# Three quads of score blocks in place of four in the attention layer of a four-layer graph network

## The chip, the cores and the metric

The program runs on one core of one Trainium2 chip. The metric is the device time of one launch in microseconds (us), the median of three runs. The core's engines are TensorE (PE in the rows: matrix products), VectorE (DVE), ScalarE (ACT), GpSimd (POOL, idle here) and SyncE (SP), which issues the transfers.

## The reference, cut to what matters

Four layers work on `x` (4096 rows of 256 features) and one dense adjacency matrix of 4096 x 4096. Each normalises its input first and adds its output to `x`. The change concerns the last one, a graph attention:

```
h   = inp @ W
e   = leaky_relu(h @ a1 + (h @ a2).T, 0.2)              # 4096 x 4096 scores, u_i + v_j
att = softmax(where(adj > 0,  e, -1e12), axis=1)
neg = -softmax(where(adj > 0, -e, -1e12), axis=1)
out = elu(concat(att @ inp, neg @ inp) @ wtrans)
```

`inp` is the normalised and clipped `x`. Everything is computed in float32 in this layer.

## The kernel before, in words

The first three layers and the preparation of the fourth take the first 1396 us of the execution. The attention then goes over eight chunks of 512 output rows (`NC = 8`, `CH = 512`). A chunk has two passes: quads 0 to 7 for the softmax of the scores, quads 8 to 15 for that of the negated scores (`QPH = 8`, `QPC = 16`). A quad covers four tiles of 128 input rows, so it is four score blocks of 128 x 512 float32 that lie side by side (8 KB in each partition). Every quad is made and used in the same place, in five steps:

1. ScalarE, `scores` (L683): four instructions that put the leaky sum of `u` and `v` into the four blocks.
2. VectorE (L1102): subtracts the row's shift.
3. VectorE (L1118): adds the mask exponents, which are zero or hugely negative.
4. ScalarE (L691): the exponential.
5. TensorE (L1370): 16 products of 128x128 by 128x257, which the trace shows as 32 records. They add to four banks of PSUM. The 257th column sums the exponentials.

The blocks come from a ring of quads, `quads`. Before step 1 may write into a quad of the ring, TensorE must have ended the products of the quad that used it last: that is the wait for `p_used` in `scores`. ScalarE's order is fixed by the code: the exponential of quad k, then the scores of quad k + 2, then the exponential of quad k + 1, and so on.

Other work stands between these steps, in written order:

- VectorE, between steps 2 and 3 of a quad, runs one search for the largest or smallest score in half a row of `adj` (L1016, L1020). There are 16 a chunk. Quads 0 to 4 serve rows of the next chunk, with that numbering shifted so that quads 11 to 15 already serve the chunk after it. At quad 3 it waits for a row load that SP issues behind a mask load. The last chunk has no searches, and the one before it none from quad 11.
- VectorE has a few more pieces of work in a chunk: the reciprocals of the row sums at quad 3 (of the chunk before) and quad 11, the sum of the two halves at quad 5 (L1061, L1063), the residual at quad 8 (L1072, L1073), and the next chunk's shifts in front of quad 11 (L1031 to L1042).
- ScalarE converts masks (L426 with `big<-big`) after the scores in quads 0, 1 and 10 to 15, scales results at quads 3 and 11 (L653), copies two rows at quads 6 and 14, and runs the three ELU instructions at quad 6 (L660, L661, L663), between the scores of quad 8 and the exponential of quad 7.
- TensorE spreads two columns over the partitions (L1221, 1.78 us) in front of quads 4 and 12.
- SP issues mask loads (L343) and row loads (L346) in one fixed sequence. A mask load waits until ScalarE has converted the mask that its buffer held, and all that stands behind it in the sequence waits with it.

Of the kernel before, what the change touches and what calls it, by code (L numbers as in the profile page):

```python
# [21 lines left out]
P = 128  # L22


def gnn_stack(nc, x_in, adj_t, adj, w_gcn, b_gcn, w_conv1, w_conv2, w_gcn2, b_gcn2,
# [7 lines left out]
    CH = 512  # L33
# [8 lines left out]
    YW = F + 1  # L42
    QD = 4
    QPH = NT // QD
    QPC = 2 * QPH
# [18 lines left out]
    with ctx:  # L64
        def sb(name, shape, dt):
            return ctx.enter_context(nc.sbuf_tensor(name, shape, dt))
# [5 lines left out]
        Y_WORDS = NT * 2 * YW  # L72
        big = sb("big", [P, Y_WORDS + NT * CH], f32)
        feat = sb("feat", [P, NT * F], f32)
        work = sb("work", [P, 10240], f32)

        def words(t, lo, n):
            return t[:, lo:lo + n]
# [21 lines left out]
        Yb = words(big, 0, Y_WORDS).rearrange("p (j s f) -> p j s f", j=NT, s=2)  # L100
# [2 lines left out]
        wt_sb = words(work, 8192, 1024).rearrange("p (k f) -> p k f", k=FB)  # L103
        t_row = words(work, 0, 4096)
        quads = [words(t, lo, QD * CH).rearrange("p (s n) -> p s n", s=QD)
                 for t, lo in ((work, 4096), (work, 4096 + QD * CH), (big, Y_WORDS + 12288), (big, Y_WORDS + 14336))]
        RING = len(quads)
        R = words(work, 8192, 2 * TPC * F).rearrange("p (s t f) -> p s t f", s=2, t=TPC)
        rows = words(feat, 0, 2 * HALF).rearrange("p (s n) -> p s n", s=2)
# [38 lines left out]
        ps = ctx.enter_context(nc.psum_tensor("ps", [P, 8, 512], f32))  # L148
# [47 lines left out]
        def wait(eng, s, v):  # L196

            if not isinstance(v, int) or v > 0:
                eng.wait_ge(s, v)
# [224 lines left out]
        def _(act):  # L424
# [202 lines left out]
            def rows_copy(s, n):  # L627

                act.wait_ge(ab_ps_ready, n)
                copy(AB[:, 2 * s:2 * s + 2, :], ps[:, 4 * s:4 * s + 2, :]).then_inc(ab_ready, 1)  # L630
# [14 lines left out]
            def averages(c, s):  # L645

                act.wait_ge(rz_ready, c * 2 + (s + 1))
                if s == 0:
                    wait(act, fin_out, c * 16)
                else:  # L650
                    wait(act, fin_ready, c)
                for t in range(TPC):
                    nc.scalar.activation(R[:, s, t, :], ps[:, 4 * s + t, 0:F], ACT.Copy, scale=rz[:, s, t:t + 1])\  # L653
                      .then_inc(att_evac, 1)
# [18 lines left out]
            def scores(c, k):  # L673

                s, q = k // QPH, k % QPH
                slots = quads[k % RING]
                if q == 0:
                    act.wait_ge(ab_ready, c * 2 + s + 1)
                if not (isinstance(c, int) and c == 0 and k < RING):
                    act.wait_ge(p_used, c * QPC + (k - RING + 1))  # L680
                for t in range(QD):
                    j = q * QD + t
                    ins = nc.scalar.activation(slots[:, t, :], AB[:, 2 * s, :], ACT.Prelu, bias=v_col[:, j:j + 1],  # L683
                                               alpha=ALPHA)
                ins.then_inc(edge_ready, 1)

            def att_chunk(c, first, last):
                for k in range(QPC):
                    act.wait_ge(lin_ready, c * QPC + k + 1)
                    slots = quads[k % RING]  # L690
                    nc.scalar.activation(slots, slots, ACT.Exp, scale=1.0 if k < QPH else -1.0).then_inc(p_ready, 1)  # L691
                    if k == 3 and not first:
                        averages(c - 1, 1)
                    if k == 6:
                        wait(act, lin_ready, c * QPC)
                        rows_copy(1, c * 2 + 2)
                    if k == QPH + 3:
                        averages(c, 0)
                    if k == QPC - 2 and not last:
                        rows_copy(0, c * 2 + 3)  # L700
                    if k + 2 < QPC:
                        scores(c, k + 2)
                    elif not last:
                        scores(c + 1, k + 2 - QPC)
                    if first and k + 2 < QPH:
                        mask_exponents(c, k + 2)
                    if not first and k < 2:
                        mask_exponents(c, k + QPH - 2)
                    if not last and QPH + 2 <= k:
                        mask_exponents(c + 1, k - QPH - 2)  # L710
                    if k == 6 and not first:
                        elu_exp(c - 1)
                    if k == QPH and not first:
                        store_result(c - 1)
                        load_x3(c)
# [23 lines left out]
        def _(dve):  # L739
# [85 lines left out]
            for c in range(NC):  # L825
                for g in range(GROUPS):
# [17 lines left out]
                    if g in (6, 8, 10, 12):  # L844
                        t = (g - 6) // 2
# [140 lines left out]
            for c in range(NC):  # L986
                dve.wait_ge(vb_evac, c + 1)
                nc.vector.tensor_reduce(vext[:, 0, c:c + 1], t_row[:, c * CH:(c + 1) * CH], AX.X, ALU.max)
                ins = nc.vector.tensor_reduce(vext[:, 1, c:c + 1], t_row[:, c * CH:(c + 1) * CH], AX.X, ALU.min)
# [99 lines left out]
            def att_chunk(c, ch, first, last):  # L1089
                for k in range(QPC):  # L1090
                    s, q = k // QPH, k % QPH
                    slots = quads[k % RING]
                    if k == SHIFT and not last:
                        shifts(c + 1, ch)
                    if q == 0:
                        dve.wait_ge(ab_ready, c * 2 + (s + 1))
                    found = searches(c, k, first, last)
                    for c_m, m in found:
                        if m % 2 == 0:
                            dve.wait_ge(row_in[m // 2 % 2], (c_m * TPC + m // 4) * 16 + 16)  # L1100
                    dve.wait_ge(edge_ready, c * QPC + k + 1)
                    nc.vector.tensor_tensor(slots, slots, AB[:, 2 * s + 1:2 * s + 2, :].to_broadcast([P, QD, CH]),  # L1102
                                            ALU.subtract).then_inc(shifted, 1)
                    for c_m, m in found:
                        dve.wait_ge(row_used, c_m * SEARCHES + m)
                        extreme(m // 4, m // 2 % 2, m % 2)
                    if k == 3 and not first:
                        reciprocals(c - 1, 1, ch)
                    if k == QPH + 3:
                        reciprocals(c, 0, ch)  # L1110
                    if k == 5 and not first:
                        summed(c - 1, ch)
                    if k == QPH and not first:
                        with_residual(c - 1, ch)
                    if s == 0:
                        dve.wait_ge(mask_ready, c * NC + (q + 1))
                    dve.wait_ge(shifted, c * QPC + k + 1)
                    nc.vector.tensor_tensor(slots, slots, mask[:, q * QD:(q + 1) * QD, :],  # L1118
                                            ALU.add if s == 0 else ALU.subtract).then_inc(lin_ready, 1)
# [36 lines left out]
            for t in range(TPC):  # L1156
# [3 lines left out]
                ins = nc.vector.tensor_tensor(D, D, M, ALU.add)  # L1160
# [5 lines left out]
        def _(pe):  # L1166
            mm = nc.tensor.matmul
# [3 lines left out]
            for k in range(FB):  # L1171
                for f in range(FB):
                    ins = mm(ps[:, 3, 2 * k:2 * k + 2], w3t_sb[:, f, k * P:(k + 1) * P], a_sb[:, f, :],
                             start=(f == 0), stop=(f == FB - 1))
# [18 lines left out]
            for c in range(NC):  # L1193
# [5 lines left out]
                for g in range(GROUPS):  # L1199
                    pe.wait_ge(cast16_done, c * GROUPS + g + 1)  # L1200
                    for jj in range(PANELS):
                        for t in range(TPC):
                            ins = mm(deg[:, t:t + 1], piece16[:, g % 2, jj, t * P:(t + 1) * P], ones16[:, :],
                                     start=False, stop=False, skip_group_check=True)
# [19 lines left out]
            for l in range(4):  # L1224
# [80 lines left out]
                if l == 3:  # L1305

                    pe.wait_ge(wa_ready, 1)
                    for k in range(2):
                        for f in range(FB):
                            ins = spread(ps[:, 4, k * F + f * P:k * F + (f + 1) * P], wa_sb[:, f, k:k + 1])  # L1310
# [46 lines left out]
            def att_chunk(c, last):  # L1357
                for k in range(QPC):
                    s, q = k // QPH, k % QPH
                    if q == 0:  # L1360
                        pe.wait_ge(ab_ready, c * 2 + (s + 1))
                    if k == 4:
                        spread_rows(1, c)
                    if k == QPH + 4 and not last:
                        spread_rows(0, c + 1)
                    pe.wait_ge(p_ready, c * QPC + k + 1)
                    for jj in range(QD):
                        j = q * QD + jj
                        for t in range(TPC):
                            ins = mm(ps[:, 4 * s + t, 0:YW], quads[k % RING][:, jj, t * P:(t + 1) * P], Yb[:, j, s, :],  # L1370
                                     start=(j == 0), stop=(j == NT - 1), skip_group_check=True)
                    ins.then_inc(p_used, 1)

# [3 lines left out]
            for c in range(NC):  # L1377
                if c >= 2:
                    pe.wait_ge(vb_evac, c - 1)
                for t in range(TPC):  # L1380
                    ins = spread(ps[:, 6 + c % 2, t * P:(t + 1) * P], uv_sb[:, c * TPC + t, 1:2])
# [5 lines left out]
            for j in range(NT):  # L1387
# [3 lines left out]
                if j == NT // 2:  # L1391
                    pe.wait_ge(hsum_ready, 1)
                    for k in range(FB):
                        ins = mm(ps[:, 5, :], hsum1[:, k:k + 1].to_broadcast([P, P]), wt_sb[:, k, :],
                                 start=(k == 0), stop=(k == FB - 1), skip_group_check=True)
# [40 lines left out]
```

## Time and profile before

| | |
|---|---|
| median of 3 runs | 2328.44 us (2327.26 to 2329.3) |
| the profiled execution | 2330.11 us, its span 2328.3 us |
| TensorE's matmuls | busy 2146.7 us, 92% of the span |
| VectorE | busy 1428.3 us, 61% |
| ScalarE | busy 1530.4 us, 66% |
| chain that ended last | TensorE 84%, transfers 7%, VectorE 5% |

Busy shares are means over layers with different limits. For the change only the stretch from 1396 us to 2318 us counts. The times in the rows are from the start of the span. An instruction on VectorE or ScalarE can begin a little before the one ahead of it has ended, so the pace of an engine is read from start to start.

### The profile page before, as it was taken

How to read it: one execution, taken by the hardware profiler on the slowest of the kernel's cores; microseconds unless marked ns; L12 is line 12 of the kernel's file. 1: busy time of each engine (PE TensorE's matmuls, PEld its weight loads, DVE VectorE, ACT ScalarE, POOL GpSimd, SP SyncE). 2: the span in 40 equal slices, each digit the busy share in tenths (PEclk: the TensorE clock that was granted, in tenths of full speed). 3: DMA queues.
4: the chain of work that ended last, by engine and by line, in shares of the span. 5: the costliest groups of instructions: out<-in, count | busy, mean ns of one | idle time of the engine just before them, and what ended most of it. 6: DMA issues, size and time to landing. Idle time of an engine off the chain costs nothing.

```text
span 2328.3 us, 27448 instructions
## 1 busy us (share of the span) xinstructions
PE 2146.7 (92%) x10872; PEld 1475.1 (63%) x10980; DVE 1428.3 (61%) x2241; ACT 1530.4 (66%) x1780; POOL 1.9 (0%) x12
## 2 busy tenths in 40 slices
PE   2665899999998999999999869999999999999998
PEld 1332455555555555554555528888888888888887
DVE  4777543410001423342444869999999999999774
ACT  6777555565655756556665447878787969696974
POOL 0000000000000000000000000000000000000000
PEclk9876999999999999999999989999999999999999
DMA  8999111310003011032112465445444535352300
GB/s 292 314 314 322 52 53 53 109 55 19 19 10 109 1 55 55 28 115 74 54 34 84 143 219 199 165 143 180 138 170 145 172 136 181 127 194 96 109 19 9
DMA packets 152992, 277.29 MB, mean 119 GB/s; under 512 B 6688, under 2 KB 79136, under 8 KB 144672
## 3 DMA queue, kind: packets, MB, share of 16 engines
q1 hardware_dynamic: 144416, 267.15, 33.8%
q10 hardware_dynamic: 8448, 8.39, 1.1%
q8 instruction: 86, 1.41, 0.2%
q14 instruction: 42, 0.34, 0.0%
HBM read 241.96 MB, written 33.55 MB: 118 GB/s over the span
## 4 chain that ended last, share of the span: by engine, by line
PE 84%; DMA 7%; DVE 5%; ACT 2%; issue 2%; POOL 0%; DVEq 0%; SPq 0%; ACTq 0%; POOLq 0%
PE ps L1370 37%; PE ps L1243 35%; PE ps L1268 8%; DMA work<-in_adj_t 6%; PE ps L1188 2%; ACT work L426 1%; PE ps L1221 1%; DVE feat L1016 1%; DMA feat<-in_adj 1%; PE ps L1253 1%; DVE feat L1020 1%; DVE hsum L1004 0%; PE ps L1343 0%; DVE big L829 0%; ACT big L426 0%
## 5 line engine op out<-in xcount | busy, mean ns | idle before, releaser
L1243 PE MATMUL ps<-work,feat 128*128 128x512 bf16 x3686 | 815.7, 379 | 11.3 <-DVE feat L876 4.3
L426 ACT ACTIVATE work<-big 128x1024 bf16<-128x1024 uint8 x472 | 496.1, 1055 | 265.2 <-PE ps L1243 261.6
L1243 PEld LDWEIGHTS ps<-work,feat 128*128 128x128 f16 x3776 | 369.1, 98 | 446.7 <-issue 6.8
L1370 PE MATMUL ps<-big,work 128*128 128x257 f32 x2048 | 451.8, 381 | 17.9 <-ACT work L691 17.9
L1370 PE MATMUL ps<-big 128*128 128x257 f32 x2048 | 449.4, 380 | 2.9 <-ACT big L691 2.9
L1370 PEld LDWEIGHTS ps<-big,work 128*128 128x128 f32 x2048 | 389.0, 191 | 74.1 <-issue 18.7
L1370 PEld LDWEIGHTS ps<-big 128*128 128x128 f32 x2048 | 388.3, 190 | 58.9 <-ACT big L691 3.7
L1268 PE MATMUL ps<-work 128*128 128x256 f32 x896 | 199.0, 379 | 4.5 <-ACT work L426 4.5
L1268 PEld LDWEIGHTS ps<-work 128*128 128x128 f32 x896 | 169.9, 190 | 32.0 <-ACT work L426 6.5
L426 ACT ACTIVATE work<-work 128x1024 bf16<-128x1024 f32 x129 | 134.6, 1052 | 80.2 <-DMA work<-in_adj_t 52.8
L691 ACT ACTIVATE work<-work 128x2048 f32<-128x2048 f32 x64 | 122.2, 1910 | 87.7 <-DVE work L1118 87.7
L691 ACT ACTIVATE big<-big 128x2048 f32<-128x2048 f32 x64 | 122.0, 1906 | 78.2 <-DVE big L1118 77.4
L907 DVE TENSOR_REDUCE gmax<-work 128x1 f32<-128x256 f32 x32 | 11.8, 414 | 263.3 <-ACT work L529 263.3
L683 ACT ACTIVATE big<-feat 128x512 f32<-128x512 f32 x256 | 163.1, 710 | 15.5 <-PE ps L1370 15.5
L683 ACT ACTIVATE work<-feat 128x512 f32<-128x512 f32 x256 | 163.3, 712 | 10.0 <-PE ps L1370 9.5
L917 DVE SCALAR_TENSOR_TENSOR work<-ps,dsc,work 128x256 f32<-128x256 f32 x64 | 31.0, 484 | 226.0 <-PE ps L1268 224.3
L1102 DVE TENSOR_TENSOR work<-work,feat 128x2048 f32<-128x2048 f32 x64 | 146.2, 2285 | 34.1 <-ACT work L683 33.6
L1102 DVE TENSOR_TENSOR big<-big,feat 128x2048 f32<-128x2048 f32 x64 | 146.3, 2285 | 23.4 <-ACT big L683 17.9
L1016 DVE CUSTOM_DVE_ANT_0 feat<-feat,work 128x2048 uint8<-128x2048 f32 x64 | 146.2, 2284 | 4.3 <-DMA feat<-in_adj 3.8
L426 ACT ACTIVATE work<-ps 128x1024 f32<-128x1024 f32 (+1 forms) x64 | 61.0, 954 | 131.3 <-PE ps L1268 111.2
L1118 DVE TENSOR_TENSOR work<-work,big 128x2048 f32<-128x2048 f32 x64 | 146.3, 2286 | 0.5
L1020 DVE CUSTOM_DVE_ANT_0 feat<-feat,work 128x2048 uint8<-128x2048 f32 x64 | 146.2, 2285 | 0.5
(147 smaller groups left out, 1479.6 us busy)
## 6 DMA issues: line engine op xcount, KB each, us to landing
work<-in_adj_t SPq DMA_DIRECT2D x128, 512.0 KB, 5.4
feat<-in_adj SPq DMA_DIRECT2D x64, 1024.0 KB, 7.2
big<-in_adj_t SPq DMA_DIRECT2D x64, 1024.0 KB, 5.3
h_spill<-work SPq DMA_DIRECT2D x32, 512.0 KB, 4.2
feat<-h_spill SPq DMA_DIRECT2D x32, 512.0 KB, 4.1
x_spill<-work SPq DMA_DIRECT2D x24, 512.0 KB, 3.0
work<-in_x SPq DMA_DIRECT2D x16, 512.0 KB, 5.3
work<-x_spill SPq DMA_DIRECT2D x16, 512.0 KB, 3.9
```

What stands on the lines that cost most here:

```text
L426: return nc.scalar.activation(out_, in_, ACT.Copy, **kw)
L683: ins = nc.scalar.activation(slots[:, t, :], AB[:, 2 * s, :], ACT.Prelu, bias=v_col[:, j:j + 1], alpha=ALPHA)
L691: nc.scalar.activation(slots, slots, ACT.Exp, scale=1.0 if k < QPH else -1.0).then_inc(p_ready, 1)
L917: nc.vector.scalar_tensor_tensor(y_t, o_t, dsc[:, bass.ds(i0 + t, 1)], bias_row, ALU.mult, ALU.add).then_inc(out_used[l], 1)
L1016: nc.vector.tensor_tensor_reduce(out=junk, in0=rows[:, h, :], in1=t_row[:, h * HALF:(h + 1) * HALF], scale=1.0, scalar=0.0, op0=ALU.mult, ...
L1020: nc.vector.tensor_tensor_reduce(out=junk, in0=rows[:, h, :], in1=t_row[:, h * HALF:(h + 1) * HALF], scale=1.0, scalar=-1.0, op0=ALU.subtr ...
L1102: nc.vector.tensor_tensor(slots, slots, AB[:, 2 * s + 1:2 * s + 2, :].to_broadcast([P, QD, CH]), ALU.subtract).then_inc(shifted, 1)
L1118: nc.vector.tensor_tensor(slots, slots, mask[:, q * QD:(q + 1) * QD, :], ALU.add if s == 0 else ALU.subtract).then_inc(lin_ready, 1)
L1188: ins = mm(ps[:, bank + f, :], parts[:, j, h, f * P:(f + 1) * P], stage0[:, n % 2, jj, :], start=(j % (NT // 2) == 0 and h == 0), stop=(j ...
L1243: ins = mm(ps[:, bank + f, :], parts[:, j, h, f * P:(f + 1) * P], stage[:, g % STAGES, jj, :], start=(fresh and h == 0), stop=(end and h = ...
L1268: ins = mm(out_slot(t), T_sb[:, k, t * P:(t + 1) * P], w_sb[:, k, :], start=(k == 0), stop=(k == KB[l] - 1), skip_group_check=True)
L1370: ins = mm(ps[:, 4 * s + t, 0:YW], quads[k % RING][:, jj, t * P:(t + 1) * P], Yb[:, j, s, :], start=(j == 0), stop=(j == NT - 1), skip_gro ...
```

## The change

The ring gets three quads; the fourth one, at the end of `big`, is no longer used. Since 16 quads a chunk are not a multiple of three, the place of a quad in the ring is now counted over all chunks. The wait in `scores` follows the ring's length: the scores of quad k + 2 now wait for the products of quad k - 1, where they waited for those of quad k - 2.

```
-                 for t, lo in ((work, 4096), (work, 4096 + QD * CH), (big, Y_WORDS + 12288), (big, Y_WORDS + 14336))]
+                 for t, lo in ((work, 4096), (work, 4096 + QD * CH), (big, Y_WORDS + 12288))]
...
             def scores(c, k):
 
                 s, q = k // QPH, k % QPH
-                slots = quads[k % RING]
+                slots = quads[(c * QPC + k) % RING]
                 if q == 0:
                     act.wait_ge(ab_ready, c * 2 + s + 1)
-                if not (isinstance(c, int) and c == 0 and k < RING):
+                if c * QPC + k >= RING:
                     act.wait_ge(p_used, c * QPC + (k - RING + 1))
```

The three other uses of `quads[k % RING]`, in ScalarE's, VectorE's and TensorE's loops, become `quads[(c * QPC + k) % RING]` in the same way. No instruction is added, removed or moved.

ScalarE's first quads of the attention, before (L683 scores, L691 exponential, L426 mask; "big" and "work" are the tensors that hold the blocks):

```order
568 L683 ACTIVATE big<-feat 128x512 x4
569 L426 ACTIVATE big<-big 128x2048 [waits mask_in1]
570 L691 ACTIVATE big<-big 128x2048 [waits lin_ready]
571 L683 ACTIVATE work<-feat 128x512 [waits p_used]
572 L683 ACTIVATE work<-feat 128x512 x3
```

And the same place now:

```order
568 L683 ACTIVATE work<-feat 128x512 [waits p_used]
569 L683 ACTIVATE work<-feat 128x512 x3
570 L426 ACTIVATE big<-big 128x2048 [waits mask_in1]
571 L691 ACTIVATE big<-big 128x2048 [waits lin_ready]
572 L683 ACTIVATE work<-feat 128x512 [waits p_used]
```

The scores of quad 3 are now the first that wait for TensorE, and they go into the first block of the ring; the sequence of the instructions is the same.

## Rows read from the trace of the kernel before

**Rows 1.** Chain that ended last, in order of time: start us, us, what.
```profile
1831.54 1.78 PE ps L1221 x16
1833.32 55.48 PE ps L1370 x256
...
2234.15 83.23 PE ps L1370 x384
```
**Rows 2.** Timeline, one quad to the next: start us, us, engine, line, operation.
```profile
1798.58 2.29 DVE L1102 TENSOR_TENSOR work<-work,feat 128x2048 f32<-128x2048 f32 x1
...
1805.20 2.28 DVE L1102 TENSOR_TENSOR big<-big,feat 128x2048 f32<-128x2048 f32 x1
1805.32 1.91 ACT L691 ACTIVATE work<-work 128x2048 f32<-128x2048 f32 x1 [2.25 <-DVE work L1118]
```
**Rows 3.** Timeline, VectorE's further work at quads 11, 3, 5 and 8.
```profile
1811.82 0.15 DVE L1031 TENSOR_TENSOR feat<-feat 128x4 f32<-128x4 f32 x1
...
1813.16 2.29 DVE L1102 TENSOR_TENSOR big<-big,feat 128x2048 f32<-128x2048 f32 x1
...
1817.57 0.16 DVE L1048 TENSOR_TENSOR feat<-ps,lone 128x4 f32<-128x4 f32 x1
...
1817.86 2.26 DVE L1118 TENSOR_TENSOR big<-big 128x2048 f32<-128x2048 f32 x1
...
1872.81 0.16 DVE L1048 TENSOR_TENSOR feat<-ps,lone 128x4 f32<-128x4 f32 x1
...
1873.31 2.28 DVE L1118 TENSOR_TENSOR big<-big 128x2048 f32<-128x2048 f32 x1
...
1886.53 1.22 DVE L1061 TENSOR_TENSOR work<-work 128x1024 f32<-128x1024 f32 x1
...
1889.37 2.28 DVE L1118 TENSOR_TENSOR work<-work,big 128x2048 f32<-128x2048 f32 x1
...
1909.22 1.22 DVE L1072 SCALAR_TENSOR_TENSOR work<-feat,work 128x1024 f32<-128x1024 f32 x1
...
1911.62 2.29 DVE L1118 TENSOR_TENSOR work<-work,big 128x2048 f32<-128x2048 f32 x1
```
**Rows 4.** Timeline, quad 2 of the fifth chunk: exponential, and its products.
```profile
1866.47 1.91 ACT L691 ACTIVATE big<-big 128x2048 f32<-128x2048 f32 x1 [0.46 <-DVE big L1118]
...
1874.77 14.03 PE L1370 MATMUL ps<-big 128*128 128x257 f32 x64
```
**Rows 5.** Timeline, quads 6 and 7 of the fifth chunk: exponentials, and quad 6's products.
```profile
1898.31 1.91 ACT L691 ACTIVATE big<-big 128x2048 f32<-128x2048 f32 x1 [2.25 <-DVE big L1118]
...
1904.29 14.03 PE L1370 MATMUL ps<-big 128*128 128x257 f32 x64
...
1906.47 1.89 ACT L691 ACTIVATE big<-big 128x2048 f32<-128x2048 f32 x1
```
**Rows 6.** Timeline, start of the last chunk, where scores wait for TensorE.
```profile
2204.47 14.03 PE L1370 MATMUL ps<-big,work 128*128 128x257 f32 x64
2204.67 2.56 ACT L683 ACTIVATE big<-feat 128x512 f32<-128x512 f32 x4 [0.77 <-PE ps L1370]
...
2207.26 2.29 DVE L1102 TENSOR_TENSOR big<-big,feat 128x2048 f32<-128x2048 f32 x1 [2.25 <-ACT big L683]
```
**Rows 7.** Timeline, the row load that quad 3 of the second chunk waits for.
```profile
1513.08 2.55 ACT L683 ACTIVATE big<-feat 128x512 f32<-128x512 f32 x4
...
1517.87 0.50 SPq L346 DMA_DIRECT2D feat<-in_adj  x1
...
1525.20 2.29 DVE L1102 TENSOR_TENSOR big<-big,feat 128x2048 f32<-128x2048 f32 x1 [0.74 <-DMA feat<-in_adj]
```
**Rows 8.** Timeline, the same wait in the fifth chunk.
```profile
1868.39 2.29 DVE L1102 TENSOR_TENSOR big<-big,feat 128x2048 f32<-128x2048 f32 x1 [1.96 <-DMA feat<-in_adj]
```
**Rows 9.** Timeline, the third quad of the attention, with TensorE's wait.
```profile
1414.33 7.20 PE L1370 MATMUL ps<-big 128*128 128x257 f32 x32 [1.13 <-ACT big L691]
```
**Rows 10.** Windows: stretch, its length, busy us (count) of PE, PEld, DVE, ACT, POOL; PEclk, DMA share, GB/s.
```profile
1414.00:1423.00 9.00, 7.20 (x32) 5.99 (x32) 8.96 (x7) 6.21 (x7) 0.00 (x0) 1.00 0.66 240
```

More of the change, by code:

```diff
@@ L689, in att_chunk @@
                     act.wait_ge(lin_ready, c * QPC + k + 1)
-                    slots = quads[k % RING]
+                    slots = quads[(c * QPC + k) % RING]
                     nc.scalar.activation(slots, slots, ACT.Exp, scale=1.0 if k < QPH else -1.0).then_inc(p_ready, 1)
@@ L1091, in att_chunk @@
                     s, q = k // QPH, k % QPH
-                    slots = quads[k % RING]
+                    slots = quads[(c * QPC + k) % RING]
                     if k == SHIFT and not last:
@@ L1369, in att_chunk @@
                         for t in range(TPC):
-                            ins = mm(ps[:, 4 * s + t, 0:YW], quads[k % RING][:, jj, t * P:(t + 1) * P], Yb[:, j, s, :],
+                            ins = mm(ps[:, 4 * s + t, 0:YW], quads[(c * QPC + k) % RING][:, jj, t * P:(t + 1) * P], Yb[:, j, s, :],
                                      start=(j == 0), stop=(j == NT - 1), skip_group_check=True)
```

## The prediction, on record before the changed kernel ran

> **What bounds the kernel now.** I read the chain that ended last first, since it says whether a wait elsewhere matters at all. From 1423 us to 2317 us it is TensorE without a break: 55.48 us for eight quads, 1.78 us for a spread, again and again, and 83.23 us for the last twelve quads [rows 1]. So a quad takes TensorE 55.48 / 8 = 6.935 us, a chunk takes it 2 x (55.48 + 1.78) = 114.52 us, and any time that TensorE spends waiting in the attention is added to the end.
>
> Then I read the timeline for the engine next in line. VectorE starts one quad 6.62 us after the other [rows 2], three instructions of about 2.205 us, so 6.615 us. Its further work in a chunk, from start to start, is 1.34 and 0.29 us at quad 11, 0.50 at quad 3, 2.84 at quad 5 and 2.40 at quad 8 [rows 3], in all 7.37 us. Its chunk is thus 16 x 6.615 + 7.37 = 113.2 us of work against TensorE's 114.5. It may stand idle for only 1.3 us a chunk; beyond that the chunk grows with it, us for us. Neither engine has reserve, and what lets their uneven rhythms pass each other is the number of quads that stand finished between them.
>
> That reserve is the third thing to read. I call lead the time from the end of a quad's exponential to the start of its products. At quad 2 of the fifth chunk it is 1874.77 - (1866.47 + 1.91) = 6.4 us [rows 4]; at quad 6, behind the lump of quad 5, it is 1904.29 - (1898.31 + 1.91) = 4.1 us [rows 5]. The kernel uses several us of lead, and VectorE is hardly held back.
>
> **The change, part by part.** No instruction comes or goes, so the only term is the wait. The scores of quad k + 2 may start when TensorE has ended quad k - 1, which is when it starts quad k (or the spread in front of it). Call that start S(k).
>
> *How large the lead can then be.* In the last chunk the longer ring already binds, and its rows give the delays: the scores start 2204.67 - 2204.47 = 0.20 us after TensorE goes on to its next quad, and the shift follows 2207.26 - 2204.67 = 2.59 us behind [rows 6]. From a shift to its exponential it is 1805.32 - 1798.58 = 6.74 us with a search in between, and the exponential takes 1.91 [rows 2]. So quad k + 2 is finished at S(k) + 0.20 + 2.59 + 6.74 + 1.91 = S(k) + 11.44, and TensorE wants it at S(k) + 13.87. The lead is at most 2.43 us. Before it was 4.1 to 6.4 at the places read above, so the wait binds.
>
> *What this costs in a chunk.* Per quad VectorE gains 6.935 - 6.615 = 0.32 us of lead, and the spreads give 1.78 in front of quads 4 and 12. The lumps take it away. I follow the lead from quad 11, where it will turn out to be zero:
> - Quad 12: 0 + 1.78 + 0.32 = 2.10. Quad 13: 2.42. From quad 14 to quad 2 of the next chunk it stands at the limit, and VectorE loses 0.32 us in each of these quads, 1.6 us in all.
> - Quad 3 has a load in it. SP sends the row behind the mask load that waits for the conversion at quad 0, and that conversion stands on ScalarE behind the scores of quad 2. From the start of such scores to the row in place it was 1525.20 - 1513.08 = 12.12 us; the row was issued at 1517.87, 7.3 us before it was there [rows 7]. The scores now start at S(0) + 0.20, so the row is there at S(0) + 12.32. VectorE is free for quad 3 at S(0) + 0.20 + 2.59 + 6.62 = S(0) + 9.41: it waits 2.9 us, where it waited 0.74 to 1.96 [rows 7, 8]. Quad 3 is finished at 12.32 + 0.50 + 6.74 + 1.91 = 21.47 and wanted at 3 x 6.935 = 20.81. TensorE waits 0.66.
> - Quad 4: lead 2.10. Quad 5: 2.10 + 0.32 - 2.84, TensorE waits 0.42.
> - Quad 7: from the exponential of quad 6 to that of quad 7 ScalarE takes 1906.47 - 1898.31 = 8.16 us, with the row copy, the scores and the ELU in between [rows 5]. TensorE takes 6.94, and the lead at quad 6 is 0.32: it waits 8.16 - 6.94 - 0.32 = 0.90.
> - Quad 8: VectorE has had this time to gain, so 0.32 + 0.32 + 0.90 + 0.32 - 2.40, TensorE waits 0.54.
> - Quad 11: 0.32 x 3 - 1.34 - 0.29, TensorE waits 0.67, and the lead is zero, as assumed.
>
> The sum is 0.66 + 0.42 + 0.90 + 0.54 + 0.67 = 3.19 us a chunk. A second way gives the same: VectorE's 113.2 of work plus 1.6 plus 2.9 of idling is 117.7, which is 114.5 + 3.2. This holds for chunks 1 to 5 (counting from 0): 15.95 us. Chunk 6 has no searches from quad 11, so its last term goes: 2.52. The last chunk has no searches at all, and VectorE has 2.2 us to spare in each quad; only the ELU at quad 6 stays, between 0 and 0.9 us, and I take 0.5. Chunk 0 has none of the lumps but quad 11, and TensorE waits for VectorE in its first quads either way: 0.
>
> The sum is 19.0 us. The profiled execution would go from 2330.11 to 2349.1. It stands 1.7 us above the median, and on the median the change gives 2328.44 + 19.0 = 2347.4 us, 0.8% more.
>
> *Bounds of the terms.* The row load is the least certain. By the second way a chunk loses 113.2 + 1.6 - 114.5 = 0.3 us and the wait at quad 3 on top. If that wait stayed at the 0.74 us of before [rows 7], a chunk would lose 1.04, six of them 6.2, and with 0.5 for the last chunk the time would be 2335.1. If the load were as late as the latest of before, 1.96 against 0.74 us [rows 7, 8], each of six chunks would lose 1.2 us more than I forecast, 26.3 in all: 2354.7. I take the middle value since it is the chain of rows 7 with nothing changed but its start.
>
> *A rule against this sum.* The lead of 4.1 us and more [rows 4, 5] is what I call the reserve in use. The Trainium skill (Trainium Kernel Development and Optimization, Best Practices) asks to double-buffer for performance and names no more buffers than two; by that rule three quads suffice and the time stays at 2328.4. The lead and the 1.3 us of slack speak against it here, and I leave it as a rival.
>
> **The rivals.**
>
> 1. *The ring of three is enough.* Two quads in work and one in use would cover everything if the lumps of VectorE fell where TensorE's spreads give time. For it: over a whole chunk VectorE needs 1.3 us less than TensorE. Against it: the largest lumps (2.9 + 0.5, 2.84, 2.40) each exceed or nearly reach the limit of 2.43, and only the one at quad 5 has a spread just ahead. Time 2328, chance 0.05.
>
> 2. *Much slower: the waits feed each other.* Later scores make later mask conversions, these make later loads, and further row loads than the one at quad 3 come late; or TensorE, with five short waits in a chunk, is granted the lower clock (1.2 in place of 2.4 GHz) now and then. For the first: SP's sequence has the rows behind the masks, and a row that is 1 us later at one more quad costs up to 6 us. Against the clock: at 1414.33 TensorE started a quad behind a wait of 1.13 us, the stretch around it had it busy for only 7.20 of 9 us, and the granted clock there was 1.00 [rows 9, 10]. My waits are 0.4 to 0.9 us. Two further late rows would give 2347 + 12 = 2359. Chance of over 2357: 0.10.
>
> 3. *Faster than before.* The blocks of the fourth quad leave `big`, so a sixth of the 4096 matmul records, 683, read `work` instead (two of three quads lie there, in place of two of four). If products from `work` were faster, TensorE's chain would shorten at 683 times that difference. It decides against my waits from 19.0 / 683 = 28 ns a record, 13% of the pace of 6.935 us / 32 = 217 ns; to come out 0.2% below before it needs 35 ns. Against it: the eight quads of a half chunk, which draw equally from both tensors, keep one pace of 55.48 us, and the pairs of quads that are marked for `big` and for `work` both take 14.03 us [rows 1, 4, 6]. Time 2323, chance 0.02.
>
> 4. *A third of it.* The row at quad 3 arrives as early as before, since SP's sequence catches up in another place. For it: of the 12.12 us from scores to row only 7.3 are the transfer [rows 7]. Against it: the rest is the scores and the conversion themselves, which both stand before it still. Then the lower bound holds, 2335. Chance 0.06.
>
> **How the numbers follow.** The forecast, 2337 to 2357 us, has 0.77; rivals 1 to 4 have 0.05, 0.10, 0.02 and 0.06. The range is 2336 to 2357: it takes in nearly all between the two bounds of the row load and some us above for the last chunk and for the ELU. A measurement of this kernel can tell about 0.2%, 4.7 us, from no change. Below that by forecast is only rival 3: faster 0.02. Rival 1 is the same: 0.05. The rest, 0.93, is slower.
>
> **What the profile of the changed kernel would show.** The chain of the attention is still nearly all TensorE, but broken in chunks 1 to 6 in front of quads 3, 5, 7, 8 and 11 by VectorE and ScalarE, at 117.7 us from one chunk to the next where it was 114.5. ScalarE's scores wait for TensorE in most quads from 14 to 2, some 0.8 us each, and VectorE waits for scores there by about 0.3. The shift of quad 3 waits 2.5 to 3.5 us for its row. The granted clock stays 1.00. All durations of single instructions are as before.
>
> Wrong would be: TensorE unbroken at 114.5 us a chunk (rival 1); waits at other quads than the five; a wait at quad 3 far from 0.7 us, which would be the row load mis-sized; a lower clock in the attention; or a total outside the range with five waits of the right size in a chunk, which would put time outside the attention.

## The result, and the profile after

The changed kernel takes 2354.0 us, the median of four runs (2349.2 to 2358.7), against 2328.5 us before. The ratio is 1.011, 95% interval [1.0088, 1.0132]. Forecast were 2347.4 us and 2336 to 2357: slower, and inside the range, 6.6 us above the point. The profiled execution took 2358.71 us, 28.6 us more than that of before. One of the four later executions of the same kernel (e1 below) took 2413.7 us in a slower state of the chip, and its ratio leaves that one out.

Where the 28.6 us are is seen by cutting the execution at TensorE's first product of the attention. In the timeline that product starts at 1396.5 us before and 1402.7 us after, 6.2 us later, in layers that the change does not touch. From the first to the last product of the attention it takes 920.9 us before and 943.3 us after: 22.4 us.

The chain that ended last, from the page of the changed kernel (shares of the span, by engine and by line):

```profile
PE 67%; DVE 15%; DMA 9%; ACT 5%; issue 4%; SPq 0%; DVEq 0%; POOL 0%; ACTq 0%
```

TensorE had 84% of this chain before; the attention's unbroken piece [rows 1] is now cut by VectorE and by transfers. The timeline of chunk 2 (counted from 0) shows the cuts. Columns: start us, us, engine, line, operation, shapes, records, and in brackets the idle time ahead with what ended it. From the chunk's first product to its quad 11, and then the first products of the next chunk:

```profile
1641.45 7.10 PE L1370 MATMUL ps<-big 128*128 128x257 f32 x32
1641.65 2.56 ACT L683 ACTIVATE work<-feat 128x512 f32<-128x512 f32 x4 [0.78 <-PE ps L1370]
...
1644.12 1.89 ACT L426 ACTIVATE big<-big 128x2048 bf16<-128x2048 f32 x1
1644.24 2.29 DVE L1102 TENSOR_TENSOR work<-work,feat 128x2048 f32<-128x2048 f32 x1 [0.16 <-ACT work L683]
1645.92 1.89 ACT L691 ACTIVATE work<-work 128x2048 f32<-128x2048 f32 x1
...
1646.45 0.51 SPq L346 DMA_DIRECT2D feat<-in_adj  x1
...
1648.38 14.03 PE L1370 MATMUL ps<-big,work 128*128 128x257 f32 x64
...
1653.85 2.29 DVE L1102 TENSOR_TENSOR big<-big,feat 128x2048 f32<-128x2048 f32 x1 [2.89 <-DMA feat<-in_adj]
...
1663.03 7.20 PE L1370 MATMUL ps<-big 128*128 128x257 f32 x32 [0.62 <-ACT big L691]
...
1671.85 7.10 PE L1370 MATMUL ps<-big,work 128*128 128x257 f32 x32
...
1679.11 7.20 PE L1370 MATMUL ps<-big,work 128*128 128x257 f32 x32 [0.15 <-ACT work L691]
...
1686.14 7.10 PE L1370 MATMUL ps<-big 128*128 128x257 f32 x32
...
1693.87 7.20 PE L1370 MATMUL ps<-big,work 128*128 128x257 f32 x32 [0.63 <-ACT work L691]
...
1701.44 7.17 PE L1370 MATMUL ps<-big,work 128*128 128x257 f32 x32 [0.37 <-ACT work L691]
...
1722.81 7.20 PE L1370 MATMUL ps<-big,work 128*128 128x257 f32 x32 [0.32 <-ACT work L691]
...
1759.37 14.03 PE L1370 MATMUL ps<-big,work 128*128 128x257 f32 x64
```

The chunk lasts 1759.37 - 1641.45 = 117.92 us, where it was 114.52. The scores start 0.20 us after TensorE's new quad (1641.65), as in [rows 6]. The row is issued at 1646.45 and VectorE starts quad 3 at 1653.85: it has waited 2.89 us. TensorE then waits in front of quads 3, 5, 7, 8 and 11, and nowhere else. The brackets understate these waits, since the record of the last product runs on behind its pace. Measured from start to start, a quad of 6.94 us and a spread of 1.78 us taken off, they are 0.78, 0.32, 0.79, 0.54 and 0.48 us. Quads behind a wait also show 7.20 us in place of 7.10: TensorE loses another 0.1 us when it starts again (at quad 8, which follows a quad that waited itself, this 0.1 us is taken off too).

VectorE's row wait in quad 3 of the chunks 1 and 3 to 6, one row each from the timeline, and for chunk 3 the issue of its row:

```profile
1535.91 2.29 DVE L1102 TENSOR_TENSOR work<-work,feat 128x2048 f32<-128x2048 f32 x1 [2.89 <-DMA feat<-in_adj]
...
1764.37 0.51 SPq L346 DMA_DIRECT2D feat<-in_adj  x1
...
1773.04 2.29 DVE L1102 TENSOR_TENSOR work<-work,feat 128x2048 f32<-128x2048 f32 x1 [4.17 <-DMA feat<-in_adj]
...
1891.53 2.29 DVE L1102 TENSOR_TENSOR work<-work,feat 128x2048 f32<-128x2048 f32 x1 [3.38 <-DMA feat<-in_adj]
...
2009.23 2.29 DVE L1102 TENSOR_TENSOR big<-big,feat 128x2048 f32<-128x2048 f32 x1 [2.66 <-DMA feat<-in_adj]
...
2127.44 2.29 DVE L1102 TENSOR_TENSOR work<-work,feat 128x2048 f32<-128x2048 f32 x1 [3.18 <-DMA feat<-in_adj]
```

With the 2.89 of chunk 2 above that is 19.2 us. The chunks last 117.93, 117.92, 119.28, 118.41, 117.70 and 117.62 us. Taking each one's own row wait off leaves 115.04, 115.03, 115.11, 115.03 and 115.04 us, and 114.44 for chunk 6, whose quad 11 has no search. A chunk costs 115.0 us and its row wait, to a tenth. The row is issued 5.00 us after the chunk's first product in every one of the six (1646.45 - 1641.45; 1764.37 - 1759.37), so what differs from chunk to chunk is the transfer itself, 7.1 to 8.6 us from issue to landing.

The window over chunk 2 of the changed kernel (stretch, length; busy us and count of PE, PEld, DVE, ACT, POOL; PEclk, DMA share, GB/s):

```profile
1642.00:1760.00 118.00, 115.91 (x546) 100.35 (x545) 113.52 (x87) 92.17 (x102) 0.00 (x0) 1.00 0.45 152
```

VectorE is idle for 118 - 113.5 = 4.5 us, the 1.6 + 2.9 of the prediction, and the granted clock is 1.00. VectorE's work and idle time over a chunk, added up, are called its books below.

### The profile page after: what moved, and what is told of

Same layout as the page of the kernel before. It is cut to its first block, busy times and chain, and to the rows that moved or that the text cites. A ratio compares the mean times of both kernels' runs of the same rounds, so it can differ in the third digit from the quotient of the medians.

```text
span 2356.9 us, 27448 instructions
## 1 busy us (share of the span) xinstructions
PE 2162.3 (92%) x10872; PEld 1476.5 (63%) x10980; DVE 1430.7 (61%) x2241; ACT 1534.8 (65%) x1780; POOL 1.9 (0%) x12
## 4 chain that ended last, share of the span: by engine, by line
PE 67%; DVE 15%; DMA 9%; ACT 5%; issue 4%; SPq 0%; DVEq 0%; POOL 0%; ACTq 0%
PE ps L1243 35%; PE ps L1370 21%; PE ps L1268 8%; DMA work<-in_adj_t 6%; DVE work L1102 3%; DVE feat L1016 3%; DMA feat<-in_adj 3%; DVE work L1118 2%; ACT work L426 1%; DVE big L1102 1%; DVE feat L1020 1%; PE ps L1188 1%; DVE big L1118 1%; PE ps L1221 1%; ACT work L683 1%
## 5 line engine op out<-in xcount | busy, mean ns | idle before, releaser
L426 ACT ACTIVATE work<-big 128x1024 bf16<-128x1024 uint8 x472 | 496.2, 1055 | 266.5 <-PE ps L1243 262.8
L1370 PE MATMUL ps<-big,work 128*128 128x257 f32 x2752 | 612.2, 382 | 29.9 <-ACT work L691 29.9
L1370 PEld LDWEIGHTS ps<-big,work 128*128 128x128 f32 x2752 | 522.3, 191 | 113.1 <-issue 21.7
L1370 PE MATMUL ps<-big 128*128 128x257 f32 x1344 | 299.0, 380 | 4.4 <-ACT big L691 4.4
L1370 PEld LDWEIGHTS ps<-big 128*128 128x128 f32 x1344 | 253.8, 190 | 43.6 <-ACT big L691 7.3
L683 ACT ACTIVATE work<-feat 128x512 f32<-128x512 f32 x344 | 219.9, 712 | 60.8 <-PE ps L1370 60.5
L1102 DVE TENSOR_TENSOR work<-work,feat 128x2048 f32<-128x2048 f32 x86 | 196.7, 2288 | 63.4 <-ACT work L683 45.6
L691 ACT ACTIVATE work<-work 128x2048 f32<-128x2048 f32 x86 | 163.7, 1904 | 92.7 <-DVE work L1118 92.7
L1118 DVE TENSOR_TENSOR work<-work,big 128x2048 f32<-128x2048 f32 x86 | 196.5, 2285 | 0.6
L426 ACT ACTIVATE work<-work 128x1024 bf16<-128x1024 f32 x129 | 134.4, 1052 | 83.0 <-DMA work<-in_adj_t 57.0
L426 ACT ACTIVATE work<-ps 128x1024 f32<-128x1024 f32 (+1 forms) x64 | 61.0, 954 | 133.0 <-PE ps L1268 111.1
L1203 PE MATMUL ps<-ones,work 128*128 128x1 bf16 x1024 | 44.2, 166 | 98.7 <-ACT work L426 98.6
L829 DVE CAST big<-work 128x1024 uint8<-128x1024 f32 x128 | 88.3, 693 | 64.7 <-DMA work<-in_adj_t 51.3
L683 ACT ACTIVATE big<-feat 128x512 f32<-128x512 f32 x168 | 107.5, 712 | 27.6 <-PE ps L1370 27.5
```

The lines of the kernel that those rows point to most:

```text
L426: return nc.scalar.activation(out_, in_, ACT.Copy, **kw)
L829: nc.vector.tensor_copy(adj8[:, g * PANELS:(g + 1) * PANELS, c * CH:(c + 1) * CH], piece[:, g % NQ, :, :]).then_inc(cast8_done, 1)
L1370: ins = mm(ps[:, 4 * s + t, 0:YW], quads[(c * QPC + k) % RING][:, jj, t * P:(t + 1) * P], Yb[:, j, s, :], start=(j == 0), stop=(j == NT - ...
```

## The experiments

"Attention" is the stretch from TensorE's first to its last product in one profiled execution; "chunk" is the time from one chunk's first product to the next one's, for chunk 5, which has none of the longest row transfers (its row still takes 7.1 to 7.4 us to land, so the column scatters by 0.25 us). In the later sessions the kernel before had a median of 2329.6 us over 13 runs, and 2330.2 over 18.

| run | median us | ratio, 95% interval | attention us | chunk 5 us |
|---|---|---|---|---|
| before (ring of four) | 2328.5 | | 920.9 | 114.52 |
| changed (ring of three) | 2354.0 | 1.0110 [1.0088, 1.0132] | 943.3 | 117.70 |
| e1 changed, again | 2351.1 | 1.0090 [1.0070, 1.0110] | 942.5 | 117.90 |
| e2 four quads, the wait of three | 2348.5 | 1.0086 [1.0069, 1.0104] | 942.8 | 117.68 |
| e3 three, row loads first | 2334.7 | 1.0021 [1.0010, 1.0032] | 926.9 | 115.46 |
| e4 three, ELU split | 2352.7 | 1.0099 [1.0084, 1.0114] | 941.8 | 117.93 |
| e5 three, less in the sum | 2345.3 | 1.0071 [1.0056, 1.0086] | 936.5 | 116.74 |
| e6 four, row loads first | 2329.4 | 0.9994 [0.9985, 1.0004] | 920.9 | 114.52 |
| e7 ring of two | 3298.9 | one run | 1893.9 | 238.93 |
| e8 three, e3 and e4 together | 2335.8 | 1.0029 [1.0016, 1.0042] | 926.9 | 115.63 |

### e1: the changed kernel again

No edit.

> The changed kernel once more. In the first profile the attention, from TensorE's first to its last product, took 943.3 us against 920.9 before (+22.4), and everything ahead of it took 1403.0 against 1396.6 (+6.4). Theory: the attention's part is the change and comes back at 940 to 946; the part ahead of it is scatter of the untouched layers (phases of TensorE's clock and of transfers) and comes back anywhere from 1396 to 1403. Rival: the change slows the part ahead too, then it is again 6 us longer, and the total stays near 2354 or above.

The attention came back at 942.5 us, and the part ahead of it took 1393.9 us, less than before's. Over ten profiled executions the first product starts anywhere from 1392 to 1403 us, in the kernel before and e6 at 1396.5 and 1396.0, in the others at 1392 to 1403. The changed kernel alone spans 1393.9 to 1402.7, so the 6 us ahead of the attention in the first profile are scatter of untouched layers, not the change. The change is worth 22 us.

### e2: the wait without the smaller ring

```
-                if not (isinstance(c, int) and c == 0 and k < RING):
-                    act.wait_ge(p_used, c * QPC + (k - RING + 1))
+                if not (isinstance(c, int) and c == 0 and k < RING - 1):
+                    act.wait_ge(p_used, c * QPC + (k - RING + 2))
```

> Four quads of memory stay, in their places, but the scores of quad k + 2 wait for quad k - 1, as in a ring of three. Theory (the wait is all): the attention takes 940 to 946 us and the total is that of the changed kernel within 0.2%. Rival (the place of the blocks matters, two thirds of them in one tensor in place of half): the attention falls between 921 and 940, by what the place costs.

Attention 942.8 us, waits at the same five quads (0.89, 0.32, 0.79, 0.53, 0.48 in chunk 2). The place of the blocks is worth nothing that shows (942.5 to 943.3 us with the smaller ring); the wait is the whole change.

### e3: the row loads ahead of the mask loads

```
                     for n in range(4):
-                        if n < 2:
-                            next_mask(c + 1, n)
                         next_row((c + 1) * TPC + 2 + n // 2, n % 2)
+                        if n < 2:
+                            next_mask(c + 1, n)
```

> Ring of three; SP sends the row load that quad 3 needs ahead of the mask load in place of behind it, likewise the next one. Theory (the late row at quad 3 is VectorE's largest idle time, and idle time of VectorE beyond 1.3 us a chunk comes back us for us): the wait of 2.9 us at quad 3 goes, a chunk falls from 117.9 to about 115.3 us, the attention from 943 to 926 to 930 us, the total to about 2335. Rival (the limit on the lead is the cost, the row just shows it): TensorE's wait at quad 3 (0.8 us) goes and no more, the attention takes 938 to 940.

The attention took 926.9 us, 15.6 to 16.3 less than with the ring of three alone, for two lines in another order. The timeline of chunk 3 (counted from 0) of this kernel:

```profile
1744.81 14.03 PE L1370 MATMUL ps<-big,work 128*128 128x257 f32 x64
...
1747.61 2.29 DVE L1102 TENSOR_TENSOR big<-big,feat 128x2048 f32<-128x2048 f32 x1 [0.16 <-ACT big L683]
...
1754.61 2.29 DVE L1102 TENSOR_TENSOR work<-work,feat 128x2048 f32<-128x2048 f32 x1 [0.30 <-ACT work L683]
...
1761.72 2.29 DVE L1102 TENSOR_TENSOR work<-work,feat 128x2048 f32<-128x2048 f32 x1
1765.40 6.91 PEld L1370 LDWEIGHTS ps<-big,work 128*128 128x128 f32 x32
1765.61 7.10 PE L1370 MATMUL ps<-big,work 128*128 128x257 f32 x32
...
1795.72 7.20 PE L1370 MATMUL ps<-big,work 128*128 128x257 f32 x32 [0.42 <-ACT work L691]
```

(In the first row the chunk's two first quads stand together.) The shift of quad 3, at 1754.61, waits 0.30 us for scores and no longer for a row. TensorE takes quads 3 to 6 without a pause and waits only at quad 7, 0.58 us, and at quad 11, 0.15 us. The waits at 5 and 8, which the row did not touch, went with the one at 3. That is what VectorE's books say and what a view of five separate costs does not. Not all of the 19.2 us of row waits came back: the chunks take 115.46 us where they took 115.0 and the row wait, since VectorE's wait for scores now reaches quad 3 too.

### e4: the ELU split over two quads

Ring of three. The two ReLU instructions of the ELU move out of `elu_exp` into `elu_relu`:

```
+                    if k == 5 and not first:
+                        elu_relu(c - 1)
                     if k == 6 and not first:
                         elu_exp(c - 1)
```

> Ring of three; two of the three ELU instructions move from quad 6 to quad 5 on ScalarE, where they fit beside TensorE's quad. Naive view (each of TensorE's waits is a cost of its own): the wait of 0.8 us in front of quad 7 goes and the attention is 0.8 x 7 = 5.5 us shorter, 937 to 938. Theory (VectorE's books decide: work plus idle time): the wait at quad 7 goes and that at quad 8 grows from 0.5 to about 1.4 us; a chunk stays at 117.7 to 117.9, the attention at 940 to 944.

TensorE's quads 3 to 8 of chunk 2 in this kernel:

```profile
1660.65 7.20 PE L1376 MATMUL ps<-big 128*128 128x257 f32 x32 [0.51 <-ACT big L695]
1669.48 7.10 PE L1376 MATMUL ps<-big,work 128*128 128x257 f32 x32
1676.73 7.20 PE L1376 MATMUL ps<-big,work 128*128 128x257 f32 x32 [0.15 <-ACT work L695]
1683.77 7.10 PE L1376 MATMUL ps<-big 128*128 128x257 f32 x32
1690.70 7.10 PE L1376 MATMUL ps<-big,work 128*128 128x257 f32 x32
1699.06 7.17 PE L1376 MATMUL ps<-big,work 128*128 128x257 f32 x32 [1.27 <-ACT work L695]
```

Quad 7, at 1690.70, follows without a wait. Quad 8, at 1699.06, comes 8.36 us behind it, a wait of 1.43 us where it was 0.54. The chunk is as long as before the edit, 117.8 us: with its own row wait taken off, each of the chunks 1 to 5 takes 115.0 us here as there. The attention took 941.8 us. The naive view expected it 5.5 us shorter and is refuted, except in the last chunk. There VectorE has time to spare, and TensorE's wait at quad 7 (0.58 us and 0.1 of restart) did come back: 112.90 us in place of 113.58.

### e5: less work in the lump of quad 5

Ring of three. Three of the four instructions that add the mean term are left out in chunks 0 to 6.

```
-                for t in range(TPC):
+                for t in range(1):
                     ins = nc.vector.scalar_tensor_tensor(R[:, 0, t, :], mean_y, lone[:, bass.ds(c * TPC + t, 1)],
```

> Ring of three; of the four instructions that add the mean term behind the sum of the halves (quad 5) three are left out, in chunks 0 to 6, so VectorE has 1.2 us less to do in each of chunks 1 to 7. View A (TensorE's waits are costs of their own): the wait of 0.32 us in front of quad 5 goes, a chunk falls by 0.3 to 0.4 us, the attention to 940 to 941. Theory (VectorE's books): all of the 1.2 us comes back, a chunk falls from 117.9 to 116.7, the attention from about 942.8 to 935 to 937.

The attention took 936.5 us, 6.0 to 6.8 less than e1, e2 and the changed kernel, and chunk 5 116.74 against 117.7 to 117.9. With its own row wait taken off each of the chunks 1 to 5 takes 113.8 us in place of 115.0: VectorE's 1.2 us come back whole, though TensorE had waited only 0.32 us at this quad.

### e6: row loads first, with four quads

The edit of e3 on the kernel before.

> Ring of four with the row loads ahead of the mask loads at the start of a chunk. Theory: VectorE's wait of 0.7 to 2 us at quad 3 goes, but TensorE does not wait in the attention, so nothing is won: attention 920.9 us, a chunk 114.52, total the same as before. Rival (VectorE's idle time is worth something with four quads too): up to 5 us shorter.

Attention 920.9 us, ratio 0.9994. VectorE's row waits are gone from the list of waits and nothing is won: with four quads VectorE's idle time at quad 3 lies within what the reserve covers. The trace also weighs VectorE's work directly. With the row wait gone, the lead at quad 0 of chunks 1, 2 and 3 is 4.16, 5.51 and 6.86 us, and from chunk 4 on 7.51: VectorE gains 1.35 us a chunk until the ring is full, which is the 1.3 us of the prediction.

### e7: a ring of two

```
-                 for t, lo in ((work, 4096), (work, 4096 + QD * CH), (big, Y_WORDS + 12288))]
+                 for t, lo in ((work, 4096), (work, 4096 + QD * CH))]
```

> A ring of two quads. Theory: the scores of quad k + 2 wait for the products of quad k itself, and since ScalarE stands in that wait, the exponential of quad k + 1 comes only behind these scores, and in half the quads behind a mask conversion. From one quad's end to the next one's: 0.20 + 2.45 (scores) + 1.80 (conversion, half of the quads) + 1.91 (exponential) + 6.94 (products), 11.5 or 13.3 us, and the extras of quads 3, 6 and 11 on ScalarE: 201 to 206 us a chunk, the attention about 1600 us, total near 3000. If only the limit on the lead (every second quad has to be made from nothing in 11.4 us) counted, it would be 9.2 us a quad, 150 us a chunk and a total near 2600.

It took 3298.9 us, 300 us more than the larger expectation. The timeline of this kernel:

```profile
2030.00 2.56 ACT L683 ACTIVATE work<-feat 128x512 f32<-128x512 f32 x4 [9.52 <-PE ps L1370]
2032.47 1.89 ACT L426 ACTIVATE big<-big 128x2048 bf16<-128x2048 f32 x1
...
2034.27 1.89 ACT L691 ACTIVATE work<-work 128x2048 f32<-128x2048 f32 x1
...
2036.21 10.12 PE L1370 MATMUL ps<-big,work 128*128 128x257 f32 x32 [6.25 <-ACT work L691]
```

The chain is the expected one: the scores wait for TensorE, the conversion and the exponential stand behind them, and TensorE waits. Against the pace of its products TensorE waits 4.61 us in front of a quad without a conversion and 6.41 with one, the sum of the instructions (4.56 and 6.36) to 0.1 us. What the expectation missed is the products: this quad takes 10.12 us and not 7.20. Over a stretch of this kernel (same columns as the window above) the granted clock is 0.81:

```profile
1995.00:2055.00 60.00, 40.39 (x148) 32.88 (x147) 30.84 (x31) 22.47 (x26) 0.00 (x0) 0.81 0.21 69
```

The sixteen quads of a chunk take 8.6 to 10.2 us each, 35 us more in sum than at 7.20. That is nearly all of the 239 - 202 = 37 us a chunk, eight times, that the expectation missed.

### e8: both edits at once

The edits of e3 and e4, ring of three.

> Ring of three with both changes: row loads first, and two ELU instructions at quad 5. With the row loads first alone a chunk took 115.46 us, with TensorE's waits at quad 7 (0.58) and 11 (0.15). Theory (books): VectorE has about 113.2 of work and 1.6 of idle time at the limit, 114.8, and the rest of the waits moves to another quad: 115.3 to 115.5 us a chunk, attention 925.5 to 927. View A: the wait at quad 7 goes with 0.1 us of restart, 114.8 a chunk, attention 922.

The wait at quad 7 went, and 0.45 us at quad 8 and 0.33 more at quad 11 took its place. The chunk, 115.63 us, is above the expected 115.3 to 115.5 and no shorter than e3's 115.46. The attention is the same, since the last chunk, as in e4, is shorter by the 0.7 us that the others are longer in sum. View A, which expected 922, falls again.

## Why the prediction was right

**What bounds the kernel.** Right. TensorE's chain was unbroken, so its new waits are the added time, and VectorE's books decide how long they are in sum: e4 and e8 moved a wait without shortening a chunk in which VectorE has no time to spare, e5 and e3 took work or idle time off VectorE and got it back.

**The chain.** Wrong. I expected it to be still nearly all TensorE, with short breaks. In chunk 2 TensorE's products are 30% of the chain, where they were 97%, and most of the rest is VectorE. That is how it has to look when VectorE's books set the length of a chunk, and I had drawn up these books without drawing this from them.

**The limit on the lead, 2.43 us.** The mechanism was right: scores 0.20 us behind TensorE's quad, shifts 2.6 behind the scores, and VectorE held back by 0.06 to 0.4 us a quad. e2 shows that the wait alone does it. The figure holds where no mask conversion is near, 2.37 us at quads 9 to 14 of the last chunk. At quads 14 to 2 of chunks 1 to 6, where I had it at the limit, the lead is only 0.40 or 0.57 us. There the exponential stands on ScalarE behind the next scores and a mask conversion, as in the rows of chunk 2: quad 1 is finished at 1645.92 + 1.89 and used at 1648.38. I had not counted that. TensorE does not wait at those quads, so it left the sum as it was.

**The five waits.** Forecast 0.66, 0.42, 0.90, 0.54 and 0.67 us at quads 3, 5, 7, 8 and 11; found in chunks 1 and 2 are 0.78, 0.32, 0.79, 0.54 and 0.48, and 0.1 us of restart behind each, which I had not counted. The sum was forecast as 3.19 and is 3.4, of which 2.9 are the waits. At quad 3 the other chunks follow their rows: 2.05, 1.27, 0.55 and 1.06 us in chunks 3 to 6.

**The row load at quad 3.** The mechanism was right and its size a little low. Forecast was 2.9 us in each of six chunks, 17.4 in all; it was 2.66 to 4.17, 19.2 in all. In chunk 2 the row was there 12.40 us after the chunk's first product, against 12.32 forecast; the excess over the six chunks is in the longer transfers. e3 removes it and with it about 16 of the 22 us.

**The sum.** Forecast 15.95 + 2.52 + 0.5 = 19.0 us; measured 22.4. The difference is 1.8 us of later rows, 0.2 in the last chunk, where TensorE waited 0.58 us at quad 7 and lost 0.1 in starting again, and about 1.5 us that the chunks 1 to 6 cost above the forecast and their row wait, 0.2 to 0.3 us each. The restarts, 0.5 us a chunk, may be behind that part, but no run separates them, and time that TensorE loses need not lengthen a chunk that VectorE sets (last section). Its cause stays open. The rest of the gap to the first median, 2354.0 against 2347.4, is not in the attention: the part ahead of it scatters by some us, and the second session gave 2351.1.

**The rivals.** That three quads are enough (rival 1) is refuted here by 22 us with three and by some 970 us with two. The Trainium skill (Trainium Kernel Development and Optimization, Best Practices) asks to double-buffer so that transfers overlap with compute. The runs speak against reading this as a depth that suffices for a ring between two engines; what the page says of transfers they do not test. Rival 3, the place of the blocks, is refuted by e2. Rival 4 is refuted by the row's 2.66 to 4.17 us. Of rival 2 two small parts came true. Further rows are late at quad 13, by 0.26 to 1.14 us in the changed kernel, at a cost of at most 0.1 us a chunk, since this is where the lead is being limited anyway. And the clock, which was forecast to stay at 1.00, did fall once in the attention (below).

What stays open: why the row of chunk 3 takes longer to land than the others, 8.6 us against 7.1 to 7.9 (4.17 us of wait), with 1.9 to 2.1 us of TensorE's waiting at that quad in all five kernels with three quads or their wait and the old order of loads. Before, one row of the six was as odd, by 1.2 us [rows 8], but a chunk later.

No version beat the kernel before. e3 is the nearest with 8 KB a partition less: 0.2% slower.

## What to carry to other kernels

When two engines are both near 99% busy, the depth of the ring between them is worth whatever lets their uneven rhythms pass each other, and a shorter ring is paid in idle time of the producer. Count that engine's work and idle time over a whole period instead of adding up the waits of the consumer: a wait that is moved is not saved (e4, e8), and a microsecond of the producer is saved even where the consumer waited only 0.3 us (e5). Where the producer has time to spare it is the other way round, and the consumer's wait is the cost (the last chunk of e4). Look also at what stands behind the newly waiting instruction in its own queue; here that was a mask conversion, behind it a row load, and putting the row load first gave back three quarters of the loss.

## What the runs showed of the hardware

**Short waits and the clock.** Waits of TensorE of 0.15 to 1.5 us between quads of 6.94 us left the granted clock at 1.00. Behind the wait of 2.05 us at quad 3 of chunk 3, the longest of chunks 1 to 7 in the changed kernel, it fell to the lower level, 1.2 GHz, for part of a quad, which took 8.89 us in place of 7.20 (timeline row, and the window around it):

```profile
1782.22 8.89 PE L1370 MATMUL ps<-big,work 128*128 128x257 f32 x32 [1.89 <-ACT work L691]
```
```profile
1781.00:1791.00 10.00, 8.78 (x33) 7.40 (x34) 10.00 (x6) 6.98 (x10) 0.00 (x0) 0.83 0.32 105
```

It fell in three of five such executions, after waits of 2.02 to 2.06 us from start to start, and did not in two, after 1.88 and 1.95 us. The length of the wait does not decide it alone: in front of quad 3 of chunk 0 TensorE waits 2.01 to 2.02 us in every kernel but the ring of two, and the clock stayed at 1.00 in all nine. In the ring of two, with waits of 4.6 or 6.4 us in front of nearly every quad, it fell again and again (0.81 over the 60 us of e7's window).

**A slow quad that cost nothing.** The 1.7 us lost to the clock there are not in the sum. With it, the chunk took 115.1 us and its row wait, its neighbours without it 115.0: while TensorE was slow, VectorE went on, the waits at quads 5 and 8 were gone in that chunk, and those at quads 7 and 11 fell to 0.58 and 0.12 us. The chunk belongs to VectorE, so TensorE's loss went into its own waits.
